# Batch 2's projections ahead of batch 0's values: a new order for one core's attention and feed-forward kernel

## The chip, the cores and the metric

The kernel runs on one core of a Trainium2 chip. The metric is device time in microseconds (us) of one execution, taken as a median over runs. Profile rows come from one profiled execution; us in them count from the start of its span.

## What is computed

Four batches (B = 4) of 512 tokens, H = 512. Each goes through cross-attention and then a feed-forward block whose weights and activations are rounded to 8-bit integers with one shared exponent per 32 numbers:

```python
query  = ctx @ Wq.T + bq ; key = ctx @ Wk.T + bk          # ctx: (4, 512, 256), 128 wide
attn   = softmax(query @ key.T)                           # (512, 512) per batch
x      = x + layernorm(x) @ attn.T                        # x: (4, 512, 512)
h      = bf16(layernorm(layernorm(x)) * ln_w + ln_b)
h      = bf16(quant(h) @ quant(W1).T + b1)                # 2048 wide
h      = bf16(gelu(h))
h      = bf16(quant(h) @ quant(W2).T + b2)                # 512 wide
out    = x + bf16(bf16(layernorm(x)) + h)
```

## The kernel before, in words

Each engine has a hand-written program; semaphores are the only order between them. A batch's tokens are 4 tiles of 128 rows (`t`), its attention 4 tiles of 128 x 512. Names are (batch, tile). The steps that matter, by engine:

- **TensorE (PE).** `context(b)` (L724) transposes the context; ScalarE's `context(b)` copies it out. `queries_keys(b)` (L732) makes both projections, 8 fp32 matmul rows of the profile; ScalarE's `query_key(b, a)` copies each out with its bias. `energies(b, t)` (L742) makes one tile of scores in one of two PSUM buffers and so waits for the `exp` of the tile two before. `values(b, t)` (L749) makes one output tile of the attention: 12 f16 matmuls (high and low parts) and an fp32 one (L761); its tile 0 waits for the transposes of all four attention tiles of the batch, each tile for the transpose of x's tile. `keep_busy(n)` (L709) multiplies the identity by itself into an unused buffer.
- **VectorE (DVE).** `negmax(b, t)` (L1031) takes the row maximum of an energy tile; `recip` and `recip_scaled` (L1036, L1040) the softmax's scale; `p_low` and `x_low` (L1045, L1050) the low halves of attention and x; `x_stats` mean and variance. Between these it quantizes the weights, one 128 x 2048 unit of W1 and of W2 per batch: `w_amax` (L862), `w_over` (L905), `w_clip`, `w_mult` (L922). The order is written out in `first_front`, `front(b, ...)` and `back(b, ...)`: first_front, back(0), front(1), back(1), then a wait for both layer norm rows (`dve.wait_ge(ld_ln, 32)`), then front(2) and the rest. The rows are first used in back(2), by `times_w` (L1059) and `plus_b` (L1064).
- **ScalarE (ACT).** `exp`, `x_high` and `p_high` make the high halves; `x_plus(b, t)` (L541) moves a tile of values out of PSUM; `x_sum(2, t)` and `x_square(2, t)` make batch 2's statistics; `load_w1(u)` and `load_w2(u)` (L533, L537) start the 1 MB loads of the next weight unit on ACT's own DMA queue, each when `w_over` of the unit before is done.
- **SP.** Issues the other DMAs in a written order: loads, then for each batch `front(b)` (L249): eight transposes, `x_transpose` (L236, waits for `x_low` of the tile and, from batch 1 on, for the batch before's `values` of that tile) and `p_transpose` (L242, waits for `p_low`), then `w2_transpose(b - 1)` and `w1_transpose(b)` (L272, L278), which wait for `w_mult`. SP takes one after the other: what stands behind a waiting issue waits too.
- **POOL (GpSimd).** Small factors, and in the second half residual sums.

Before the change PE's order around batch 1 is: energies (0,2) and (0,3), queries_keys(1), energies (1,0) and (1,1), context(2), values(0,0), energies(1,2), values(0,1), energies(1,3), values (0,2) and (0,3), queries_keys(2), energies (2,0) and (2,1). The two layer norm rows (256 KB each, one row broadcast to 128 partitions) are loaded on SP right behind the first weight unit, before `load_ctx(2)`.

Of the kernel before, what the change touches and what calls it, by code (L numbers as in the profile page):

```python
# [15 lines left out]
P = 128  # L16
# [13 lines left out]
def xattn_ffn_kernel(nc, x, ctx_in, wq, bq, wk, bk, ln_w, ln_b, w1, b1, w2, b2, out):  # L30
    B, L, H = x.shape
# [4 lines left out]
    LT = L // P  # L36
    NT = N // P
# [18 lines left out]
    with ExitStack() as stack:  # L56
# [20 lines left out]
        lnw = sb("lnw", [P, H], F32)  # L77
# [144 lines left out]
        def _(sp):  # L222
# [26 lines left out]
            def front(b, ctx=None, later=None):  # L249


                x_transpose(b, 0)
                if ctx is not None:
                    load_ctx(ctx)
                p_transpose(b, 0)
                x_transpose(b, 1)
                p_transpose(b, 1)
                x_transpose(b, 2)
                p_transpose(b, 2)
                p_transpose(b, 3)  # L260
                x_transpose(b, 3)
                if later is not None:
                    load_x(later)
                if b < B - 1:
                    if b > 0:
                        w2_transpose(b - 1)
                    w1_transpose(b)
                else:
                    w1_transpose(b)
                    w2_transpose(b - 1)  # L270
# [12 lines left out]
            load_x(1)  # L283
            load_x(2)
            sp.dma_start(wst[:, W2, :], w2_t[0]).then_inc(ld_w2, 16)
            sp.dma_start(lnw[:, :], ln_w.rearrange("(o n) -> o n", o=1).broadcast_to([P, H])).then_inc(ld_ln, 16)
            sp.dma_start(lnb[:, :], ln_b.rearrange("(o n) -> o n", o=1).broadcast_to([P, H])).then_inc(ld_ln, 16)
            load_ctx(2)
            front(0)
            load_x(3)  # L290
            front(1, 3)
            front(2)
            front(3)

# [190 lines left out]
        def _(act):  # L485
# [78 lines left out]
            def v_sums(b, t):  # L564

                if t >= 2:
# [5 lines left out]
                act.activation(vs[:, LT * b + t, :], vs[:, LT * b + t, :], ACT.Copy,  # L572
                               accum_out=sums[:, 1, 0, t:t + 1]).then_inc(v_sum, 1)

            def batch(b, front, qk, v):

                for t in range(LT + 1):
                    if t < NT and (t > 0 or front == 0):  # L580
                        exp(front, t)
                        x_high(front, t)
                    if t > 0:
                        p_high(front, t - 1)
                    if b is not None and t > 1:
                        x_plus(b, t - 2)
                    if v is not None and t == 1:
                        v_out(v, 0)
                    if v is not None and t > 0:
                        v_sums(v, t - 1)  # L590
                    if v is not None and 0 < t < LT:
                        v_out(v, t)
                    if t == 2 and b is not None:
                        load_w2(front)
                    if qk is not None and t == 3:
                        context(qk)
                if front + 1 < B and b is not None:
                    load_w1(front + 1)
                if b is not None:
                    x_plus(b, LT - 1)  # L600
                if b is None:
                    act.wait_ge(w_first, 1)
                    load_w1(front + 1)
                    x_sum(2, 0)
                    x_sum(2, 1)
                if qk is not None:
                    query_key(qk, 0)
                if b is None:
                    x_sum(2, 2)
                if b is not None:  # L610
                    x1_square(b, 0)
                if qk is not None:
                    query_key(qk, 1)
                if b is None:
                    x_sum(2, 3)
                    for t in range(LT):
                        x_square(2, t)
                if b is not None:
                    x1_square(b, 1)
                    x1_square(b, 2)  # L620
                if front + 1 < B:
                    exp(front + 1, 0)
                    x_high(front + 1, 0)
                if b is not None:
                    x1_square(b, 3)

            context(0)
            act.wait_ge(ld_bqk, 32)
            query_key(0, 0)
            query_key(0, 1)  # L630
            batch(None, 0, 1, None)
            batch(0, 1, 2, None)
            for b in range(1, B - 2):
                batch(b, b + 1, b + 2, b - 1)
# [73 lines left out]
        def _(pe):  # L708
# [55 lines left out]
            def batch(b, front, qk):  # L764


                if qk is not None and b is not None:
                    context(qk)
                for t in range(LT):
                    if b == 0:  # L770
                        values(b, t)
                    if t < NT - 2:
                        energies(front, t + 2)
                    if b is not None and b > 0:
                        values(b, t)
                if qk is not None:
                    queries_keys(qk)
                    energies(qk, 0)
                    energies(qk, 1)

            context(0)
            keep_busy(3)
# [1 line left out]
            energies(0, 0)  # L784
            energies(0, 1)
            context(1)
            batch(None, 0, 1)
            pe.wait_ge(c_idx, 1)
            batch(0, 1, 2)
            for b in range(1, B - 2):  # L790
                batch(b, b + 1, b + 2)
            batch(B - 2, B - 1, None)
# [492 lines left out]
```

## Time and profile before

| what | us |
|---|---|
| median of 3 runs | 273.22 |
| lowest and highest of them | 271.6, 274.33 |
| the profiled execution, whole | 274.33 |
| its span, first to last instruction | 272.5 |

The span and the 1.83 us around it make the profiled execution's time. It is the highest of the three runs, so differences are worked out on its rows and then added to the median. TensorE's mean granted clock in it was 0.948 of full speed (2.4 GHz); the other level is half of that, 1.2 GHz.

### The profile page before, as it was taken

The page shows a single profiled execution, that of the slowest core. Times are in us where ns is not written, and L with a number is a line of the kernel's source. Part 1 is how long each engine was busy: PE and PEld are TensorE (multiplying, and loading weights), DVE is VectorE, ACT ScalarE, POOL GpSimd, SP SyncE. Part 2 cuts the span into 40 slices and gives each one's busy share as a digit, 9 for nine tenths or more (in the row PEclk, how much of TensorE's full clock was granted, in tenths as well). Part 3 has the DMA queues.
Part 4 walks back from the last instruction along what each step waited for, and adds up shares of the span by engine and source line. Part 5 has one row for each costly group of instructions (what it writes and reads, how often), then busy time and mean ns, then how long its engine had stood idle before and what let it go on. Part 6 is the DMA issues. An engine that isn't in the chain of part 4 may idle for free.

```text
span 272.5 us, 3187 instructions
## 1 busy us (share of the span) xinstructions
PE 226.3 (83%) x931; PEld 97.5 (36%) x940; DVE 243.0 (89%) x354; ACT 175.7 (64%) x303; POOL 68.1 (25%) x101
## 2 busy tenths in 40 slices
PE   6774859989995937559996797899999789999993
PEld 6432314434431413214442333344444234444431
DVE  3599964999999999999979999999999999877982
ACT  2377753669997739767789798855556554556510
POOL 2193200042007300160521200633203333333400
PEclk9996868999999986968999999999999999999999
DMA  5999999999899828693060522656650566655773
GB/s 153 373 400 291 247 163 265 285 224 224 161 262 224 165 40 219 128 195 78 0 117 0 96 49 50 110 122 135 135 132 20 119 135 140 135 129 118 157 183 123
DMA packets 103078, 42.92 MB, mean 157 GB/s; under 512 B 93845, under 2 KB 96153, under 8 KB 102553
## 3 DMA queue, kind: packets, MB, share of 16 engines
q1 hardware_dynamic: 100224, 36.45, 61.0%
q10 hardware_dynamic: 2360, 6.30, 7.5%
q0 software_dynamic: 480, 0.02, 0.1%
q8 instruction: 5, 0.08, 0.1%
q14 instruction: 9, 0.07, 0.1%
HBM read 15.48 MB, written 4.19 MB: 72 GB/s over the span
## 4 chain that ended last, share of the span: by engine, by line
DVE 50%; PE 24%; DMA 10%; ACT 7%; issue 3%; SPq 3%; POOL 2%; ACTq 0%; DVEq 0%; POOLq 0%
DVE amax L862 12%; PE ps L821 9%; PE ps L811 5%; PE ps L758 5%; DMA pT<-phl 4%; DVE pf L976 4%; DVE wquant L966 4%; DVE w_int L905 3%; DVE phl L1047 3%; DMA xhl<-pf 3%; DVE vw L1059 3%; DVE hq L1064 3%; DVE xhl L1052 3%; DVE wquant L971 2%; DVE nmax L1033 2%
## 5 line engine op out<-in xcount | busy, mean ns | idle before, releaser
L821 PE MATMUL ps<-w2T,xhl 128*128 128x512 bf16 x247 | 56.5, 379 | 8.3 <-DMA xhl<-pf 7.9
L811 PE MATMUL ps<-w1T,cxT 128*128 128x512 bf16 x256 | 58.0, 380 | 0.0
L641 ACT ACTIVATE wst<-ps 128x1024 bf16<-128x1024 f32 x32 | 32.0, 1017 | 24.3 <-PE ps L811 24.3
L862 DVE TENSOR_REDUCE amax<-phl 128x64 f32<-128x2048 bf16 x16 | 36.5, 2281 | 4.0 <-ACT phl L648 4.0
L821 PEld LDWEIGHTS ps<-w2T,xhl 128*128 128x128 bf16 x256 | 24.4, 98 | 39.0 <-DMA xhl<-pf 8.3
L811 PEld LDWEIGHTS ps<-w1T,cxT 128*128 128x128 bf16 x256 | 23.7, 98 | 32.6 <-issue 6.2
L758 PE MATMUL ps<-h1q,xT 128*128 128x512 f16 x96 | 26.5, 435 | 9.8 <-ACT xs L546 6.2
L648 ACT ACTIVATE phl<-wst 128x2048 bf16<-128x2048 bf16 x16 | 30.6, 1910 | 1.6 <-DVE wquant L966 0.5
L758 PE MATMUL ps<-pT,xT 128*128 128x512 f16 x96 | 24.5, 410 | 7.5 <-DMA pT<-phl 7.0
L471 POOL TENSOR_TENSOR wst<-wst,vs 128x512 bf16<-128x512 bf16 x12 | 15.3, 1275 | 53.2 <-DVE wquant L971 53.2
L506 ACT ACTIVATE pf<-ps,nmax 128x512 f32<-128x512 f32 x16 | 10.8, 678 | 19.5 <-DVE nmax L1033 19.4
L661 ACT ACTIVATE wst<-ps 128x512 bf16<-128x512 f32 x16 | 9.5, 596 | 19.8 <-PE ps L821 19.4
L738 PE MATMUL ps<-cxT,wqkT 128*128 128x512 f32 x32 | 17.1, 683 | 5.6 <-ACT cxT L496 5.6
L746 PE MATMUL ps<-qkT 128*128 128x512 f32 x32 | 16.5, 618 | 5.7 <-ACT qkT L500 3.3
L758 PEld LDWEIGHTS ps<-h1q,xT 128*128 128x128 f16 x96 | 10.2, 109 | 27.0 <-issue 19.9
L407 POOL TENSOR_SCALAR mean<-sums 128x4 f32<-128x4 f32 x4 | 1.9, 479 | 69.5 <-ACT xs L546 69.5
L966 DVE TENSOR_TENSOR wquant<-phl,mxi 128x2048 int16<-128x2048 bf16 x15 | 18.3, 1223 | 0.3
L976 DVE TENSOR_TENSOR pf<-wquant,mxs 128x2048 bf16<-128x2048 int16 x15 | 18.3, 1217 | 0.0
L862 DVE TENSOR_REDUCE amax<-wst 128x64 f32<-128x2048 f32 x8 | 18.2, 2280 | 0.0
L758 PEld LDWEIGHTS ps<-pT,xT 128*128 128x128 f16 x96 | 9.7, 103 | 23.2 <-issue 14.5
L761 PE MATMUL ps<-xs,ident_x 128*128 128x512 f32 x32 | 16.7, 603 | 0.0
L905 DVE TENSOR_TENSOR w_int<-wst,mxi 128x2048 int16<-128x2048 f32 x7 | 16.0, 2284 | 0.0
(90 smaller groups left out, 370.6 us busy)
## 6 DMA issues: line engine op xcount, KB each, us to landing
wst<-in_L_ffn_W ACTq DMA_DIRECT2D x6, 1024.0 KB, 6.5
xs<-in_x SPq DMA_DIRECT2D x4, 1024.0 KB, 8.0
out_x<-wst SPq DMA_DIRECT2D x16, 256.0 KB, 2.9
cx<-in_ctx SPq DMA_DIRECT2D x4, 512.0 KB, 5.7
wst<-in_L_ffn_W SPq DMA_DIRECT2D x2, 1024.0 KB, 11.3
xhl<-pf SPq DMA_TRANSPOSE x17, 4.3
lnw<-in_L_ffn_ln_w SPq DMA_DIRECT2D x1, 256.0 KB, 12.6
lnb<-in_L_ffn_ln_b SPq DMA_DIRECT2D x1, 256.0 KB, 12.2
```

What stands on the lines that cost most here:

```text
L641: act.activation(ys[:, k, 1024 * g:1024 * g + 1024], ps_y[:, 2 * g:2 * g + 2, :], ACT.Copy)\
L648: act.activation(gs[:, k, :], ys[:, k, :], ACT.Gelu_apprx_tanh).then_inc(g_rdy, 1)
L738: last = pe.matmul(ps_qk[:, a, :], wqkT[:, a, c, :], cxT[:, c, :], start=(c == 0), stop=(c == CT - 1))
L746: pe.matmul(ps_e[:, t % 2, :], qkT[:, 0, P * t:P * t + P], qkT[:, 1, :], start=True, stop=True).then_inc(e_ps, 1)
L758: pe.matmul(ps_pv[:, t % 2, :], xT[:, t, NT * a + n, :], pTs[b % 2][:, :, NT * c + n, :], start=(s == 0), stop=False)
L761: pe.matmul(ps_pv[:, t % 2, :], ident_x[:, :], xs[:, LT * b + t, :], start=False, stop=True).then_inc(pv_ps, 1)
L811: last = pe.matmul(ps_y[:, c, :], h1T[:, k, t, :], w1T[:, 4 * c:4 * c + 4, t, :], start=False, stop=(t == KT - 1))
L821: last = pe.matmul(ps_z[:, k, :], h2T[:, k, t, :], w2T[:, t, :], start=False, stop=(t == FT - 1))
L862: dve.tensor_reduce(amax[:, a, :], by_block, AX_X, ALU.max, apply_absolute_value=True)\
L905: dve.tensor_tensor(blocks(w_int[:, :]), blocks(wst[:, a, :]), inverse, ALU.mult)\
L966: dve.tensor_tensor(pairs(h2u[:, k, :]), pairs(gs[:, k, :]), per_block(mxi[:, k, :, :]), ALU.mult).then_inc(h2_step[k], 1)
L976: dve.tensor_tensor(pairs(h2q[:, k, :]), pairs(h2u[:, k, :]), per_block(mxs[:, k, :, :]), ALU.mult).then_inc(h2_step[k], 1)
```

## The change

1. PE: a list written out, `first_batches()`, takes the place of the first two calls of `batch`. `keep_busy(22)` comes behind energies(0,3). queries_keys(2) comes ahead of values(0,0), and so does energies(1,2); energies(1,3) follows values(0,0); energies (2,0) and (2,1) are laced into the last values of batch 0. The wait for the scaled identity (`c_idx`) moves to the front of the list.
2. ACT: `first_batch()` makes ScalarE's `context(2)` right behind query_key(1,1); exp, x_high of (1,0) and (1,1) and p_high(1,0) come ahead of the four `x_square(2, t)`; `query_key(2, 0)` and `(2, 1)` come behind x_plus(0,1), with a new wait for energies(1,3).
3. SP: the loads of `lnw` and `lnb` move from ahead of `load_ctx(2)` to behind `front(1, 3)`, that is behind `w1_transpose(1)`. VectorE's wait for them stays where it is, ahead of its front(2).

```diff
--- before.py
+++ after.py
@@ -283,12 +283,12 @@
             load_x(1)
             load_x(2)
             sp.dma_start(wst[:, W2, :], w2_t[0]).then_inc(ld_w2, 16)
-            sp.dma_start(lnw[:, :], ln_w.rearrange("(o n) -> o n", o=1).broadcast_to([P, H])).then_inc(ld_ln, 16)
-            sp.dma_start(lnb[:, :], ln_b.rearrange("(o n) -> o n", o=1).broadcast_to([P, H])).then_inc(ld_ln, 16)
             load_ctx(2)
             front(0)
             load_x(3)
             front(1, 3)
+            sp.dma_start(lnw[:, :], ln_w.rearrange("(o n) -> o n", o=1).broadcast_to([P, H])).then_inc(ld_ln, 16)
+            sp.dma_start(lnb[:, :], ln_b.rearrange("(o n) -> o n", o=1).broadcast_to([P, H])).then_inc(ld_ln, 16)
             front(2)
             front(3)
 
@@ -572,17 +572,43 @@
                 act.activation(vs[:, LT * b + t, :], vs[:, LT * b + t, :], ACT.Copy,
                                accum_out=sums[:, 1, 0, t:t + 1]).then_inc(v_sum, 1)
 
+            def first_batch():
+
+                for t in range(LT + 1):
+                    if t < NT:
+                        exp(0, t)
+                        x_high(0, t)
+                    if t > 0:
+                        p_high(0, t - 1)
+                    if t == 3:
+                        context(1)
+                act.wait_ge(w_first, 1)
+                load_w1(1)
+                x_sum(2, 0)
+                x_sum(2, 1)
+                query_key(1, 0)
+                x_sum(2, 2)
+                query_key(1, 1)
+                context(2)
+                x_sum(2, 3)
+                exp(1, 0)
+                x_high(1, 0)
+                exp(1, 1)
+                x_high(1, 1)
+                p_high(1, 0)
+                for t in range(LT):
+                    x_square(2, t)
+
             def batch(b, front, qk, v):
 
 
-
                 for t in range(LT + 1):
-                    if t < NT and (t > 0 or front == 0):
+                    if t < NT and t > int(b == 0):
                         exp(front, t)
                         x_high(front, t)
-                    if t > 0:
+                    if t > int(b == 0):
                         p_high(front, t - 1)
-                    if b is not None and t > 1:
+                    if t > 1:
                         x_plus(b, t - 2)
                     if v is not None and t == 1:
                         v_out(v, 0)
@@ -590,45 +616,34 @@
                         v_sums(v, t - 1)
                     if v is not None and 0 < t < LT:
                         v_out(v, t)
-                    if t == 2 and b is not None:
+                    if t == 2:
                         load_w2(front)
-                    if qk is not None and t == 3:
+                    if b == 0 and t == 3:
+                        act.wait_ge(e_ps, 2 * NT)
+                        query_key(2, 0)
+                        query_key(2, 1)
+                    if b > 0 and qk is not None and t == 3:
                         context(qk)
-                if front + 1 < B and b is not None:
+                if front + 1 < B:
                     load_w1(front + 1)
-                if b is not None:
-                    x_plus(b, LT - 1)
-                if b is None:
-                    act.wait_ge(w_first, 1)
-                    load_w1(front + 1)
-                    x_sum(2, 0)
-                    x_sum(2, 1)
-                if qk is not None:
+                x_plus(b, LT - 1)
+                if b > 0 and qk is not None:
                     query_key(qk, 0)
-                if b is None:
-                    x_sum(2, 2)
-                if b is not None:
-                    x1_square(b, 0)
-                if qk is not None:
+                x1_square(b, 0)
+                if b > 0 and qk is not None:
                     query_key(qk, 1)
-                if b is None:
-                    x_sum(2, 3)
-                    for t in range(LT):
-                        x_square(2, t)
-                if b is not None:
-                    x1_square(b, 1)
-                    x1_square(b, 2)
+                x1_square(b, 1)
+                x1_square(b, 2)
                 if front + 1 < B:
                     exp(front + 1, 0)
                     x_high(front + 1, 0)
-                if b is not None:
-                    x1_square(b, 3)
+                x1_square(b, 3)
 
             context(0)
             act.wait_ge(ld_bqk, 32)
             query_key(0, 0)
             query_key(0, 1)
-            batch(None, 0, 1, None)
+            first_batch()
             batch(0, 1, 2, None)
             for b in range(1, B - 2):
                 batch(b, b + 1, b + 2, b - 1)
@@ -764,19 +779,35 @@
             def batch(b, front, qk):
 
 
-                if qk is not None and b is not None:
+                if qk is not None:
                     context(qk)
                 for t in range(LT):
-                    if b == 0:
-                        values(b, t)
                     if t < NT - 2:
                         energies(front, t + 2)
-                    if b is not None and b > 0:
-                        values(b, t)
+                    values(b, t)
                 if qk is not None:
                     queries_keys(qk)
                     energies(qk, 0)
                     energies(qk, 1)
+
+            def first_batches():
+
+                energies(0, 2)
+                energies(0, 3)
+                keep_busy(22)
+                queries_keys(1)
+                context(2)
+                energies(1, 0)
+                energies(1, 1)
+                queries_keys(2)
+                energies(1, 2)
+                values(0, 0)
+                energies(1, 3)
+                values(0, 1)
+                values(0, 2)
+                energies(2, 0)
+                values(0, 3)
+                energies(2, 1)
 
             context(0)
             keep_busy(3)
@@ -784,9 +815,8 @@
             energies(0, 0)
             energies(0, 1)
             context(1)
-            batch(None, 0, 1)
             pe.wait_ge(c_idx, 1)
-            batch(0, 1, 2)
+            first_batches()
             for b in range(1, B - 2):
                 batch(b, b + 1, b + 2)
             batch(B - 2, B - 1, None)
```

## Rows read from the trace of the kernel before

**Rows 1.** The page: busy time by engine; DMA share in 40 slices of the span.
```profile
PE 226.3 (83%) x931; PEld 97.5 (36%) x940; DVE 243.0 (89%) x354; ACT 175.7 (64%) x303; POOL 68.1 (25%) x101
...
DMA  5999999999899828693060522656650566655773
```
**Rows 2.** Waits of DVE, whole span: us in total, times, longest.
```profile
DVE nmax L1033 <- PE ps L746: 5.2, 1, 5.2
...
DVE rinv L1038 <- ACT pf L506: 0.6, 1, 0.6
DVE phl L1047 <- ACT phl L512: 0.6, 1, 0.6
```
**Rows 3.** Timeline of PE, 0 to 60: start, duration, what, idle before it.
```profile
4.85 1.23 PE L712 MATMUL ps<-ident 128*128 128x128 f32 x8
...
24.00 6.20 PE L738 MATMUL ps<-cxT,wqkT 128*128 128x512 f32 x8 [5.08 <-ACT cxT L496]
...
37.41 5.28 PE L758 MATMUL ps<-h1q,xT 128*128 128x512 f16 x12 [3.58 <-DMA h1q<-phl]
...
55.91 3.60 PE L738 MATMUL ps<-cxT,wqkT 128*128 128x512 f32 x8
```
**Rows 4.** Windows: busy us of PE, PEld, DVE, ACT, POOL; TensorE's granted clock, DMA share, GB/s.
```profile
24.00:30.20 6.20, 6.20 (x8) 2.34 (x8) 6.17 (x16) 3.24 (x8) 0.00 (x0) 0.59 1.09 262
37.41:43.64 6.23, 6.23 (x15) 2.63 (x16) 1.83 (x5) 0.56 (x1) 0.00 (x0) 0.57 1.20 207
...
8.00:24.00 16.00, 9.45 (x33) 4.29 (x31) 13.92 (x29) 10.47 (x19) 9.60 (x19) 0.95 1.06 387
```
**Rows 5.** Timeline of DVE: negmax (1,0), (1,2), (1,3); w_mult(W1,1), w_amax(W1,2), w_mult(W1,2).
```profile
33.02 0.68 DVE L1033 TENSOR_REDUCE nmax<-ps 128x1 f32<-128x512 f32 x1
...
44.54 0.69 DVE L1033 TENSOR_REDUCE nmax<-ps 128x1 f32<-128x512 f32 x1 [5.23 <-PE ps L746]
...
48.93 0.68 DVE L1033 TENSOR_REDUCE nmax<-ps 128x1 f32<-128x512 f32 x1
...
58.07 1.23 DVE L922 TENSOR_TENSOR wquant<-w_int,mxs 128x2048 bf16<-128x2048 int16 x1
...
63.52 2.29 DVE L862 TENSOR_REDUCE amax<-wst 128x64 f32<-128x2048 f32 x1
...
83.81 1.20 DVE L922 TENSOR_TENSOR wquant<-w_int,mxs 128x2048 bf16<-128x2048 int16 x1
```
**Rows 6.** Timeline of SP: lnw, lnb, x_transpose(1,3), w1_transpose of units 1, 2 and 3.
```profile
10.23 1.25 SPq L286 DMA_DIRECT2D lnw<-in_L_ffn_ln_w  x1
11.52 0.64 SPq L287 DMA_DIRECT2D lnb<-in_L_ffn_ln_b  x1
...
58.72 4.30 SPq L239 DMA_TRANSPOSE xT<-xhl  x1
...
64.91 3.25 SPq L274 DMA_TRANSPOSE w1T<-wquant  x1
...
89.11 2.78 SPq L274 DMA_TRANSPOSE w1T<-wquant  x1
...
117.44 2.50 SPq L274 DMA_TRANSPOSE w1T<-wquant  x1
```
**Rows 7.** DMA issues: KB each, us from issue to landing; the last is x_transpose(1,3).
```profile
wst<-in_L_ffn_W ACTq DMA_DIRECT2D x6, 1024.0 KB, 6.5
...
out_x<-wst SPq DMA_DIRECT2D x16, 256.0 KB, 2.9
...
xT<-xhl SPq DMA_TRANSPOSE x1, 6.5
```
**Rows 8.** Timeline of ACT: the issue of load_w1(2).
```profile
56.74 0.39 ACTq L535 DMA_DIRECT2D wst<-in_L_ffn_W  x1
```
**Rows 9.** DMA busy share in tenths, 30 to 50 and 50 to 70, slices of 0.5 us.
```profile
DMA  9799999899999999979900997999939964999959
...
DMA  9948969899399999967799999199999999999989
```

## The prediction

> **What bounds the kernel now.** I read the page first: DVE is busy 89% of the span, and the 16 DMA engines, though a mean over the whole span hides it, nearly all of the first third [rows 1]. Next the waits of DVE, because an engine this full sets the end wherever it does not wait. Up to the second half it has one large hole, 5.2 us at a negmax that waits for energies; two small ones of 0.6 us follow, one for an exp of batch 1 and one for a p_high of batch 2 [rows 2]. From PE's timeline the hole is plain: energies(1,2) stands behind values(0,0), and that waits for batch 0's attention transposes until 37.41 [rows 3]. It then runs at a granted clock of 0.57, mostly the lower level of 1.2 GHz, after 3.58 us of idle: 6.23 us from 37.41 to 43.64 [rows 4]. The chain of waits says the same: transposes, values, energies, negmax, and from there DVE nearly without a break to the feed-forward half. So what moves DVE's work behind 40 us moves the end, one for one.
>
> The second thing to see is SP and the DMA queue. Weight loads on ACT's queue and transposes on SP's hold each other up: a 1 MB weight load takes 6.5 us, and x_transpose(1,3), issued 2 us after load_w1(2) [rows 8], held SP for 4.30 us and landed after 6.5 us [rows 6, 7]. The change puts two loads behind these and leaves DVE's wait for them where it was.
>
> **Part 1: the energies in front.** energies(1,2) needs exp(1,0), whose negmax runs at 33.02 [rows 5], so it can be done at about 35 if PE has the projections of batch 2 behind it by then. DVE asks for it, without the hole, at 44.54 - 5.23 - 0.6 = about 38.7. The two holes of 5.23 and 0.61 us go: 5.84 us [rows 2], and ACT's exp(1,0), no longer behind four x_square, is what closes the small one.
>
> Next late would be energies(1,3), now behind values(0,0). DVE wants it 48.93 - 44.54 = 4.4 us after negmax(1,2) (p_low, x_low and a w_over lie between) [rows 5], at 43.1. values(0,0) can begin at 35.9 to 37.4 (transposes landing as before, or 1.4 us sooner, part 3) and takes about 6.23 x 0.57 = 3.6 us at the full clock, or 6.2 as now: its end is 39.5 to 43.6, and energies(1,3) follows at once. So it costs nothing warm and up to 1.5 us cold. I take nothing, by the next part.
>
> **Part 2: identities and batch 2's projections.** 22 identities at 1.23/8 = 0.154 us are 3.4 us [rows 3]. They lie in PE's 5.08 us wait for the copied context and delay nothing; at half the clock they would take 6.8 and push the projections by 1.7. What they may give: queries_keys(1) took 6.20 us at a granted clock of 0.59, while the same eight rows take 3.60 warm [rows 3, 4]. Those 2.6 us do not reach DVE by themselves, since negmax(1,0) stands behind a w_amax until 33.02. They make room for queries_keys(2), which moves in front of energies(1,2). If both are warm, PE is through them by about 33.6, ahead of exp(1,0). If the clock stays low, they end near 39, energies(1,2) comes at 40 and energies(1,3) at 47: DVE waits again for 1.5 and then some 2.7 us. Value taken: warm, 0; bounds 0 and 4.2. The new ACT wait for energies(1,3) stands behind exp(1,3), which needs that tile anyway, so it is met when reached; queued behind it are query_key(2) and p_high(1,3), which DVE needs only for its last p_low of the stage. The moved wait for the scaled identity is met before PE gets there. Both: 0.
>
> **Part 3: the rows loaded later.** In front they leave 0.5 MB fewer in a stretch that moves 387 GB/s [rows 4]: 0.52/387 = 1.4 us, by which the first transposes can land sooner. DVE does not wait for those any more: 0, from 0 to -1.4 for PE. Their two issues (1.89 us) end long before SP's next wait opens: 0.
>
> Behind, all counts. DVE ends w_mult(W1,1) at 59.2 (the next instruction's start) and reaches the wait for the rows at 63.5, 4.3 us later [rows 5]. SP passes w1_transpose(1), which needs the same w_mult, at 64.91 + 3.25 = 68.16, that is 9.0 us after it, because x_transpose(1,3) and w2_transpose(0) had to get through beside the load of W1 first [rows 6]. Then lnw's issue, 1.25, and 256 KB from lnb's issue to landing. For that I take 2.9, a store of the same size [rows 6, 7]. Landing is 9.0 + 1.25 + 2.9 = 13.2 us after w_mult, and DVE has been waiting since 4.3: a new stall of 8.9 us. All of this moves with DVE (w_mult and, through w_over, the W1 load that blocks the queue), so the 5.84 does not shorten it. Behind the waiting DVE instruction stands all of front(2): w_amax, x_low, negmax(2,2), and so ACT's exp(2,2), SP's transposes of batch 2, PE's values(2).
>
> Bounds of the stall: with the shortest w1 transpose issue (2.50) right after w_mult, lnb's 0.64 for each issue and 2.9 to land, 2.50 + 0.64 + 2.9 = 6.0, less 4.3: 1.7 us. At the other end the landing takes 6.5, as a transfer beside a weight load does [rows 7]: 8.9 + 3.6 = 12.5. I stay with 8.9, since this very queue state is in the trace.
>
> One more term: the DMA engines must do the same work in less time. Between 40 and 70 the half-us digits leave about 4 us idle, 1.0 of it at 40 to 41 [rows 9]; with the 1.4 us from the front that is 5.4 us of slack for a shift of 5.84. I put 0.6 us on the landing, bounds 0 and 3.
>
> The Trainium skill speaks against this part. In "DMA: Bandwidth & Descriptors", section Rules for kernel authors, it advises to issue a DMA early and to wait on its semaphore late; the old place does, and the new one issues late for a wait that did not move. Its section Issuing engines are not separate DMA queues says that DMAs of all issuing engines share the same 16 DMA engines, which agrees with the 6.5 us of a transpose beside ACT's load [rows 7]. Its figures in Anatomy of one DMA, fitted to transfers issued by GpSimd (2.0 us fixed plus bytes over 436 GB/s), would make an estimate of 2.6 us for lnb, and the sum 0.3 us smaller.
>
> **Sum.** -5.84 + 8.9 + 0.6 = +3.7; the 0.6 us hole of batch 2 goes too, since ACT is ahead after DVE's stall: -0.6. That is +3.1 us, 277.4 for the profiled execution's 274.33. That execution is 1.1 us over the median, so the forecast is 273.22 + 3.1 = 276.3. I count on nothing later to absorb it: what DVE waits for after that hangs on its own p_low and x_low of batches 2 and 3.
>
> **Rivals.**
> 1. *Faster: the queue is clear when w_mult ends.* The rows decide from the point where lnb lands within 4.3 + 5.84 = 10.1 us of w_mult(W1,1); forecast is 13.8. For it: a lone w1 transpose takes 2.50, and PE is through values(0) earlier than it must be. Against it: every 1 MB load on ACT's queue has a blocked transpose beside it. At the lower bound, -5.84 + 1.7 = -4.1: 269.1; halfway, 271.
> 2. *Even: the backlog is that of batch 2.* There w_mult ended at 85.0 and w1_transpose at 89.11 + 2.78 = 91.9, 6.9 us later instead of 9.0 [rows 5, 6]. Then 3.1 - 2.1 = +1.0: 274.2.
> 3. *Slower still: PE stays cold, or the landing is long.* queries_keys(2) ahead of values(0,0) becomes a load on the path: up to 4.2 us more, or 3.6 for the landing: 279.9 to 280.5. For it: clock 0.59 and 0.57 in just these stretches [rows 4]. Against it: 22 identities close most of the idle time before them.
>
> **How the numbers follow.** A change of this kernel under 1%, 2.7 us, can hardly be told from none. Forecast's own case, 0.50: its spread of -2 to +2 about 276.3 crosses the 1% line at 275.95, so 0.30 slower and 0.20 same. Rival 1, 0.20: 0.18 faster, 0.02 same. Rival 2, 0.17, same. Rival 3, 0.13, slower. Together faster 0.18, same 0.39, slower 0.43. The range of 8 in 10 reaches into rivals 1 and 3: 269.8 to 279.5. The forecast's own range is 274.3 to 278.3.
>
> **What would show it.** Right: no wait of DVE for energies at negmax(1,2); a new one of about 9 us ahead of w_amax(W1,2), released by the DMA of lnb, with DVE's w_amax(W1,2) at 66 to 67.5; SP's lnw issue 9 us after w_mult(W1,1); queries_keys(1) and (2) at about 3.6 us with the clock at 1.0. Wrong: lnb landed when DVE comes to its wait, or a stall there of less than 5 us (rival 1); a DVE wait at negmax(1,2) or (1,3) and a clock near 0.6 in PE's 24 to 41 (rival 3).

## The result, and the profile after

The changed kernel takes 280.9 us, median of four runs, against 273.36 for the kernel before: ratio 1.0264, 95% interval 1.018 to 1.0348. The forecast was 276.3, with a range up to 279.5: the sign was right, the size not. Ratios and their intervals, here and below, leave out executions that stand apart from the rest of their kernel's; medians and ranges hold them all. The four executions run from 279.29 to 291.96, and that spread is a finding of its own (questions 1 and 3 below). The profiled execution is the lowest of them: 279.29 us, its span 277.5 against 272.5, so +5.0 where +3.1 was forecast for it. Of the other three there is no trace.

DVE's largest wait after (us in total, times, longest), and DVE's timeline with negmax (1,2) and (1,3), w_mult(W1,1) and w_amax(W1,2):

```profile
DVE amax L892 <- DMA lnb<-in_L_ffn_ln_b: 12.0, 1, 12.0
```
```profile
38.57 0.69 DVE L1063 TENSOR_REDUCE nmax<-ps 128x1 f32<-128x512 f32 x1
...
42.95 0.68 DVE L1063 TENSOR_REDUCE nmax<-ps 128x1 f32<-128x512 f32 x1
...
52.10 1.23 DVE L952 TENSOR_TENSOR wquant<-w_int,mxs 128x2048 bf16<-128x2048 int16 x1
...
69.61 2.29 DVE L892 TENSOR_REDUCE amax<-wst 128x64 f32<-128x2048 f32 x1 [12.04 <-DMA lnb<-in_L_ffn_ln_b]
```

Against [rows 5], negmax(1,2) is 44.54 - 38.57 = 5.97 us earlier, and so is w_mult(W1,1): the hole is gone and nothing took its place up to here. DVE reaches its wait for the rows at 69.61 - 12.04 = 57.57, 5.95 us ahead of before, and leaves it 69.61 - 63.52 = 6.09 us behind. About 1.1 us of that is given back later, half of it in the 0.6 us at phl of batch 2, which is gone [rows 2].

PE's timeline answers to [rows 3], its windows (columns as in [rows 4]) to the granted clock:

```profile
18.77 5.07 PE L727 MATMUL ps<-ident 128*128 128x128 f32 x44
24.06 3.67 PE L753 MATMUL ps<-cxT,wqkT 128*128 128x512 f32 x8 [0.22 <-ACT cxT L496]
...
30.33 3.60 PE L753 MATMUL ps<-cxT,wqkT 128*128 128x512 f32 x8
...
36.25 2.75 PE L773 MATMUL ps<-h1q,xT 128*128 128x512 f16 x12 [0.50 <-DMA h1q<-phl]
...
39.70 1.02 PE L761 MATMUL ps<-qkT 128*128 128x512 f32 x2
```
```profile
24.06:27.73 3.67, 3.67 (x10) 1.71 (x11) 3.63 (x9) 3.08 (x8) 0.00 (x0) 1.00 0.90 203
...
36.25:39.00 2.75, 2.75 (x13) 1.43 (x14) 2.68 (x6) 2.75 (x8) 0.00 (x0) 1.00 1.18 192
```

Both projections take 3.6 to 3.7 us, the 12 f16 matmuls of values(0,0) 2.75 us (5.28 before), at a granted clock of 1.00 (2.4 GHz). PE does what the change says.

So the loss is in the wait, and its inside is SP. SP's timeline after, from x_transpose(1,0) on; the row with x2 is the pair p_transpose (1,2) and (1,3), the row behind it the second of the pair by itself. Then x_transpose(1,0), the pair and its second in before:

```profile
39.96 1.23 SPq L239 DMA_TRANSPOSE xT<-xhl  x1
...
51.03 6.27 SPq L246 DMA_TRANSPOSE pT<-phl  x2
52.40 4.89 SPq L246 DMA_TRANSPOSE pT<-phl  x1
57.39 1.25 SPq L239 DMA_TRANSPOSE xT<-xhl  x1
58.69 2.12 SPq L280 DMA_TRANSPOSE w2T<-wquant  x1
60.85 3.26 SPq L274 DMA_TRANSPOSE w1T<-wquant  x1
64.15 0.58 SPq L290 DMA_DIRECT2D lnw<-in_L_ffn_ln_w  x1
64.78 0.43 SPq L291 DMA_DIRECT2D lnb<-in_L_ffn_ln_b  x1
```
```profile
43.74 1.23 SPq L239 DMA_TRANSPOSE xT<-xhl  x1
...
55.41 3.22 SPq L246 DMA_TRANSPOSE pT<-phl  x2
57.40 1.23 SPq L246 DMA_TRANSPOSE pT<-phl  x1
```
ACT's load_w1(2) after, beside [rows 8]:
```profile
50.76 0.39 ACTq L535 DMA_DIRECT2D wst<-in_L_ffn_W  x1
```

Read the shifts, not the times. DVE is 5.97 us earlier, and load_w1(2), which follows it, 56.74 - 50.76 = 5.98. SP is not: its front(1) begins with x_transpose(1,0), which waits for values(0,0) on PE, and that is only 43.74 - 39.96 = 3.8 us earlier. So the load of W1 comes earlier in SP's row. In both kernels one transpose is still issued in the usual time behind it (1.23 us before, 1.33 after), and the next one is held until 6.3 and 6.5 us after the load's issue. Before, the load started between the two of the pair, and the one held was x_transpose(1,3) (4.30 us [rows 6]); two transposes of weights were left, 5.1 us. After, it starts ahead of the pair, the one held is the second of the pair (4.89 us), and x_transpose(1,3) is left as well: 6.8 us. So x_transpose(1,3) starts only 1.3 us earlier than before, and w1_transpose(1) ends at 64.11, 4.05 earlier. That is 10.9 us after w_mult, where 9.0 had been taken over from before.

### The profile page after: what moved, and what is told of

Same layout as the page of the kernel before. It is cut to its first block, busy times and chain, and to the rows that moved or that the text cites. A ratio compares the mean times of both kernels' runs of the same rounds, so it can differ in the third digit from the quotient of the medians.

```text
span 277.5 us, 3276 instructions
## 1 busy us (share of the span) xinstructions
PE 234.5 (85%) x975; PEld 102.8 (37%) x984; DVE 242.7 (87%) x354; ACT 176.0 (63%) x303; POOL 67.3 (24%) x101
## 4 chain that ended last, share of the span: by engine, by line
DVE 59%; PE 19%; DMA 8%; SPq 5%; ACT 3%; issue 3%; POOL 2%; DVEq 0%; POOLq 0%; ACTq 0%
DVE amax L892 14%; PE ps L851 9%; PE ps L841 5%; DVE w_int L935 5%; DVE pf L1006 4%; DVE wquant L996 4%; DVE phl L1077 4%; DVE xhl L1082 4%; DMA xhl<-pf 3%; DVE nmax L1063 3%; DVE vw L1089 3%; DVE hq L1094 3%; DVE wquant L1001 2%; DVE wquant L952 2%; SPq L246 2%
## 5 line engine op out<-in xcount | busy, mean ns | idle before, releaser
L841 PE MATMUL ps<-w1T,cxT 128*128 128x512 bf16 x256 | 59.7, 388 | 0.0
L773 PE MATMUL ps<-pT,xT 128*128 128x512 f16 x96 | 27.8, 450 | 13.4 <-ACT xs L546 7.1
L773 PE MATMUL ps<-h1q,xT 128*128 128x512 f16 x96 | 25.6, 422 | 4.8 <-ACT xs L546 4.3
L471 POOL TENSOR_TENSOR wst<-wst,vs 128x512 bf16<-128x512 bf16 x12 | 15.4, 1284 | 53.2 <-DVE wquant L1001 53.2
L506 ACT ACTIVATE pf<-ps,nmax 128x512 f32<-128x512 f32 x16 | 10.9, 681 | 25.9 <-DVE nmax L1063 25.8
L761 PE MATMUL ps<-qkT 128*128 128x512 f32 x32 | 18.4, 676 | 7.7 <-ACT pf L506 6.0
L773 PEld LDWEIGHTS ps<-pT,xT 128*128 128x128 f16 x96 | 10.5, 112 | 32.6 <-issue 26.0
L546 ACT ACTIVATE xs<-ps,mr 128x512 f32<-128x512 f32 x16 | 10.8, 675 | 7.1 <-PE ps L776 7.1
```

Of the source, the lines that this page charges most:

```text
L471: pool.tensor_tensor(ws[:, k, :], zs[:, k, :], vs[:, i, :], ALU.add).then_inc(zv_rdy, 1)
L761: pe.matmul(ps_e[:, t % 2, :], qkT[:, 0, P * t:P * t + P], qkT[:, 1, :], start=True, stop=True).then_inc(e_ps, 1)
L773: pe.matmul(ps_pv[:, t % 2, :], xT[:, t, NT * a + n, :], pTs[b % 2][:, :, NT * c + n, :], start=(s == 0), stop=False)
L841: last = pe.matmul(ps_y[:, c, :], h1T[:, k, t, :], w1T[:, 4 * c:4 * c + 4, t, :], start=False, stop=(t == KT - 1))
```

## The experiments

| run | what | executions | median, range (us) | ratio to before, 95% |
|---|---|---|---|---|
| after_again | the kernel after | 4 | 290.57, 284.64–293.79 | 1.0644, 1.0559–1.0728 |
| rows_front | after, rows at their old place | 10 | 272.49, 270.29–273.07 | 0.9928, 0.9899–0.9956 |
| rows_only | before, rows late | 4 | 278.93, 278.12–280.31 | 1.0191, 1.0128–1.0253 |
| wait_late | after, DVE's wait late | 6 | 278.68, 274.28–279.75 | 1.0206, 1.0155–1.0257 |
| old_order_wait_late | before, rows and wait late | 4 | 270.31, 270.23–271.16 | 0.9888, 0.9856–0.992 |
| energies_only | before, energies of batch 1 in front | 6 | 271.57, 270.27–281.27 | 0.9915, 0.9876–0.9955 |
| old_order_energies_wait_late | both of these | 11 | 271.81, 269.12–281.85 | 0.9862, 0.9833–0.9892 |
| x3_late | after, load_x(3) behind the rows | 5 | 280.73, 280.19–283.64 | 1.0254, 1.0221–1.0287 |
| x3_late_wait_late | and DVE's wait late | 10 | 272.6, 270.58–284.25 | 0.9936, 0.9892–0.998 |
| w1_load_late | after, load_w1(2) later | 4 | 286.06, 280.68–288.57 | no interval |
| w1_gated | load_w1(2) behind load_w2(1), wait late | 5 | 275.23, 271.71–282.61 | 0.9915, 0.9891–0.994 |
| loads_late | after, x(3) and context(3) loaded later | 4 | 281.22, 281.01–281.59 | 1.0277, 1.0205–1.0349 |
| loads_late_wait_late | and DVE's wait late | 10 | 271.78, 269.39–273.1 | 0.9938, 0.9901–0.9976 |
| after_beside | the kernel after | 6 | 288.75, 285.44–293.98 | 1.0591, 1.054–1.0643 |
| loads_late_beside | loads_late, same chip as after_beside | 6 | 280.81, 278.57–281.52 | 1.0274, 1.0224–1.0324 |
| loads_late_wait_late_beside | same chip | 12 | 271.53, 268.32–273.11 | 0.9908, 0.9868–0.9948 |
| rows_front_no_ident | rows_front without identities | 4 | 270.44, 269.59–271.89 | 0.9874, 0.9832–0.9916 |
| best_loads_late | and x(3), context(3) later | 4 | 269.81, 268.98–271.08 | 0.986, 0.9781–0.994 |

### Question 1: the rows or the new order?

**after_again**: nothing edited.

> The changed kernel once more, as the measure for the others. Its median was 7.5 us over before, while the two profiled spans differ by 5.0 (277.5 against 272.5). Theory A (all of the loss is DVE's 12.0 us wait for lnb, and the rest of the change gains 5.9): 278.5 to 281, with a DVE wait for lnb of 11 to 13 us. Theory B (the new order costs something besides, which the profiled execution shows less than others): 280 to 282.

290.57 us: above both ranges, and four executions over 9 us. In the trace of the lowest, 284.64 us, the wait for lnb is 16.5 us, and both weight loads of this stretch take 11 us instead of 6.7, with transposes beside them at up to 15.4 us instead of 7.4. This state of long loads and long transposes is called the jam below. The size of the loss is not one number.

**rows_front**: after, the two rows back where they were.

```diff
+            sp.dma_start(lnw[:, :], ...)
+            sp.dma_start(lnb[:, :], ...)
             load_ctx(2)
             front(0)
             load_x(3)
             front(1, 3)
-            sp.dma_start(lnw[:, :], ...)
-            sp.dma_start(lnb[:, :], ...)
```

> The changed kernel with the two layer norm loads back at their old place. Theory A: the wait of 12.0 us goes, holes of 0.6 and 0.4 us on DVE come back: 267 to 269, DVE at w_amax(W1,2) at about 57.6. Theory B: no wait for lnb either, but the end is at 271 to 274, since the order of PE and ACT loses elsewhere.

272.49, faster than before by 0.7%, as theory B had it. The whole loss hangs on the rows. But of the 5.84 us that PE's order takes out of DVE's first hole only some 2 reach the end: new waits for energies of 1.25 and 2.68 us, and 0.86 for an exp, come behind it:

```profile
44.00 0.69 DVE L1063 TENSOR_REDUCE nmax<-ps 128x1 f32<-128x512 f32 x1 [1.25 <-PE ps L761]
...
70.14 0.69 DVE L1063 TENSOR_REDUCE nmax<-ps 128x1 f32<-128x512 f32 x1 [2.68 <-PE ps L761]
```

**rows_only**: before, the rows alone moved (the same lines, the other way).

> The kernel before with nothing but the two loads moved behind w1_transpose(1). Theory A: SP passes w1_transpose(1) at 68.2 as in the kernel before, and 0.6 + 4.8 us later lnb is there: a DVE wait of 10 us from 63.5 to 73.6, 282 to 284. Theory B (the stall needs the crowd that the new order makes in the queue): a wait under 6 us, 276 to 279.

278.93, slower by 1.9%: the wait is near that of theory A, the time in the range of theory B. DVE's waits and values(0,0) on PE (timelines, its window with the granted clock), then SP:

```profile
40.55 0.69 DVE L1033 TENSOR_REDUCE nmax<-ps 128x1 f32<-128x512 f32 x1 [1.05 <-PE ps L746]
...
68.88 2.29 DVE L862 TENSOR_REDUCE amax<-wst 128x64 f32<-128x2048 f32 x1 [9.28 <-DMA lnb<-in_L_ffn_ln_b]
...
36.05 2.75 PE L758 MATMUL ps<-h1q,xT 128*128 128x512 f16 x12 [2.02 <-DMA h1q<-phl]
...
36.05:38.80 2.75, 2.75 (x13) 1.42 (x14) 2.75 (x3) 2.13 (x5) 0.00 (x0) 1.00 1.76 188
```
```profile
51.05 3.59 SPq L246 DMA_TRANSPOSE pT<-phl  x2
54.74 4.30 SPq L239 DMA_TRANSPOSE xT<-xhl  x1
...
60.99 2.51 SPq L274 DMA_TRANSPOSE w1T<-wquant  x1
```

Two things to see. The 5.2 us hole [rows 2] is down to 1.05 with PE's order untouched: with half a megabyte fewer in front of them the transposes let values(0,0) start at 36.05 instead of 37.41, after 2.02 us of idle instead of 3.58, and it then ran at a granted clock of 1.00 (2.75 us for 5.28). The earlier start is worth 1.4 us of this, the clock 2.5. And the wait is 9.28, close to the 8.9 that the forecast took from before: in the old order SP does move with DVE. There x_transpose(1,0) starts at 39.75 and load_w1(2) at 52.75, both 3.99 us earlier than before. The load starts between the two of the pair again, x_transpose(1,3) is held for the same 4.30 us, and w1_transpose ends 8.3 us after w_mult. The other traces without the jam say the same of the lag: where the load came forward by more than x_transpose(1,0), by 2.6 us in energies_only, 4.0 in rows_front_no_ident and 4.4 in rows_front (all with the rows in front), it is 11.7, 11.3 and 13.1 us.

**wait_late**: after, DVE's wait put behind its front(2), nothing on SP changed.

```diff
-            dve.wait_ge(ld_ln, 32)
             front(2, ...)
+            dve.wait_ge(ld_ln, 32)
```

> The changed kernel, loads late as it has them, but DVE's wait for them moved behind front(2), right ahead of their first use. Theory A: the loads land at about 69.5, DVE wants them about 22 us after 57.6, so no wait is left: 267 to 269, as with the loads in front. Theory B: 271 to 274.

278.68 (274.28 to 279.75), above both ranges. Three executions are at 279.5 to 279.8, which the ratio of 1.0206 stands for, three at 274.3 to 277.8. The wait for the rows is gone, and in the trace of the lowest DVE waits for a weight load instead (4.18 us once): the loads of this stretch took 10.4 and 11.3 us. So the long loads are not made by the two row loads themselves, which are issued behind them at 70, or by DVE standing still.

### Question 2: what is each part worth without the wait?

**old_order_wait_late**: before, with both of the moves above (rows late, wait late), PE and ACT as before.

> The kernel before with the rows loaded late, and DVE's wait moved to their first use. With the rows moved alone the 5.2 us hole had shrunk to 1.05, since values(0,0) began 1.4 us sooner and at full clock. Theory C: this gain stays if the wait goes, 269 to 271. Theory A (only PE's order closes the hole for good): 272 to 274.

270.31, all runs within 0.9 us, as theory C had it: faster than before by 1.1%, with none of PE's and ACT's new order. **energies_only** does nothing but swap two calls of PE in the old order:

```diff
-                    if b == 0:
-                        values(b, t)
                     if t < NT - 2:
                         energies(front, t + 2)
-                    if b is not None and b > 0:
+                    if b is not None:
                         values(b, t)
```

> The kernel before with energies(1,2) and (1,3) ahead of values (0,0) and (0,1) on PE, nothing else. If the hole is only the place of the energies: 5.2 us less on DVE up to 44, then the same crowd in the queue gives 2 to 4 of it back: 270 to 272. If the identities and batch 2's projections are needed for it: energies(1,3) waits behind a cold values(0,0), 272 to 274.

271.57, 0.85% faster, in the first of the two ranges; the identities and batch 2's projections are not needed for it. Both it and old_order_wait_late close the same hole of DVE, so they do not add up, as the run with both shows:

> The best so far (old order, rows late, DVE's wait at their first use, 270.3) and energies (1,2) and (1,3) ahead of values (0,0) and (0,1). DVE has 1.6 us left to win at negmax(1,2): 268.7 at the least if the queue keeps up; by theory E the weight loads come 1.6 us sooner and closer to what SP still has to do, so some executions fall back to 272 to 280.

**old_order_energies_wait_late**: 271.81 (269.12 to 281.85), ratio 0.9862. Five of its eleven executions are at 269.1 to 270.1, and others fall back as expected; the profiled one, 279.87, is among those, with load_w2(1) at 13.7 us and DVE waiting 3.43 and 4.30 us for weights. In this kernel load_w2(1) starts at 43.21, in old_order_wait_late, whose four executions have nothing of the kind, at 44.94. It pointed to that load.

### Question 3: what makes the loads long?

**x3_late** moves `load_x(3)` from behind front(0) to behind the rows; **x3_late_wait_late** also has the late wait.

> The changed kernel with one edit: batch 3's x, 1 MB that nobody needs before x_stats(3), is loaded behind the two rows instead of ahead of front(1). Theory C (the new order starts load_w2(1) while x(3) and the context of batch 3 are still in SP's queue; then the weight loads take 11 us instead of 6.5 and the transposes 12 to 15): all weight loads 6 to 7 us, SP through w1_transpose(1) by 60 to 62, lnb landed by 66 to 67, a DVE wait of 8 to 9 us, 275 to 278 with little spread. Theory D (two weight loads back to back block the transposes by themselves, x(3) does not matter): SP through at 64 to 71 as before, 279 to 291.

> As x3_late, and DVE's wait for the rows moved behind front(2), ahead of their first use. Theory C: no wait for lnb, weight loads at 6 to 7 us, so DVE keeps most of the 5.9 us: 267 to 270. Theory D: DVE waits for a weight load or for energies behind late transposes, 274 to 279 as without the x(3) edit.

280.73, in the range of theory D, and 272.6 (270.58 to 284.25), in neither: seven of its ten executions are at 270.6 to 274.2, three at 277.2 to 284.3. The wait for lnb is 15.8 us in the first one's trace, the loads 8.5 and 8.1: batch 3's x alone is not it.

**w1_load_late** starts load_w1(2) behind the last x1_square of batch 0, so that the two weight loads do not overlap; **w1_gated** makes ACT wait for the landing of load_w2(1) first, with the late wait.

```diff
                 if front + 1 < B:
+                    if b == 0:
+                        act.wait_ge(ld_w2, 32)
                     load_w1(front + 1)
```

> The changed kernel with one edit: ACT starts load_w1(2) behind batch 0's last x1_square (at about 58) instead of at 50.8, right after load_w2(1). Theory E (transposes get through only between two weight loads; where load_w2(1) has not landed when load_w1(2) is issued, they stay stuck through both): transposes of batch 1 out by 55, SP through w1_transpose(1) by 57 to 60, lnb landed at 62 to 64, and DVE then waits for the weights until 64 to 65.5 instead of 69.6 or 75: 274 to 277, little spread. Theory F (the DMA engines are full by volume, order is nothing): 1 MB less ahead of lnb is 2.7 us, a wait until 67 to 72: 277 to 288, the same spread.

> The kernel with DVE's late wait (274 to 280 before), and one more edit: ACT waits for load_w2(1) to land before it issues load_w1(2). Theory E: the two loads never overlap, the stuck state is gone, 270 to 274 in every execution. Theory F: the gate only delays the weights, 275 to 280 again.

286.06 and 275.23: theory E missed both, though two of the second's five executions are at 271.7 and 272.0. The times lie in theory F's ranges, but its reason does not hold either. load_w2(1) took 12.0 and 13.2 us with no second load beside it. The first one's DMA view, 40 to 55 us (40 slices of 0.375 us), with the load that was issued at 43.26:

```profile
DMA  9625899679999169999991400001111197998989
GB/s 60 27 44 109 317 382 360 202 257 415 394 311 213 40 146 316 304 287 350 339 571 47 70 25 25 25 10 41 27 23 23 14 313 271 456 494 316 317 184 194
...
wst<-in_L_ffn_W ACTq DMA_DIRECT2D x1, 1024.0 KB, 12.0
```

For 3.75 us (digits 23 to 32) the 16 engines move 10 to 70 GB/s, nine of the ten digits at 0 or 1, while this load, the context load and two transposes are outstanding. It is not a matter of volume.

**loads_late** takes both of SP's plain loads (loads that only copy, without a transpose) away from the start of load_w2(1): x(3) behind the rows, context(3) from behind x_transpose(1,0) to behind x_transpose(1,2). **loads_late_wait_late** adds the late wait.

```diff
-                if ctx is not None:
-                    load_ctx(ctx)
...
+                if ctx is not None:
+                    load_ctx(ctx)
...
-            load_x(3)
             front(1, 3)
...
+            load_x(3)
```

> The kernel after, with batch 3's x load moved behind the two rows and batch 3's context load moved from behind batch 1's first x transpose to behind the third. Theory G (the long transfers need a plain load of SP's still in flight when load_w2(1) starts at 43): now only transposes are in flight beside it, every weight load takes 6 to 7 us and every transpose of batch 1 6 to 9, SP's last weight transpose of batch 1 ends at 60 to 64, VectorE's wait for the second row is 8 to 12 us and the time 276 to 280 with runs within 2 us of each other. Theory H (a weight load and transposes alone can do it): loads of 8 to 14 us in the trace, wait of 13 to 17, runs spread over 4 us or more, 280 to 290.

> The same with VectorE's wait for the rows moved behind batch 2's front. Theory G: no wait for the rows, no wait for a weight load over 1 us, 267 to 270 us with all runs within 2 us. Theory H: weight loads of 8 to 14 us, VectorE waiting 3 to 5 us for one, and runs spread from 270 to 280.

281.22 with all four executions within 0.6 us, and 271.78 (269.39 to 273.1). Of theory G the narrow spread came true, and a short load_w2(1), 5.8 us; load_w1(2) at 7.8 us, the wait of 13.8 us and the time lie above its ranges. The second lies above theory G's time: its loads take 6.0 and 8.0 us, and DVE waits 1.24 us for a weight load and 3.16 us for x(3), which this edit itself loads late. These executions came from another chip than the wide ones, so the kernel after ran once more beside them:

> The kernel after, unchanged, on the same chip and in the same call as loads_late_beside, since its earlier executions came from other chips than loads_late's. Theory G (plain loads in flight beside load_w2(1) make the long transfers): runs spread over 5 us or more, 279 to 294. Rival K (the spread belongs to the chip, not to the kernel): as wide or as narrow as loads_late_beside.

> loads_late unchanged, beside the kernel after. Theory G: all runs within 2 us of each other, 280 to 282, whatever after does beside it. Rival K: the same spread as after_beside.

> loads_late_wait_late unchanged, on the same chip. Theory G: runs within 4 us, 269 to 273, as on the other chip. Rival K: runs up to 280 where after_beside is wide.

On one chip: after 288.75 (285.44 to 293.98), loads_late 280.81 (278.57 to 281.52), with the late wait 271.53 (268.32 to 273.11). The ranges are somewhat wider than theory G had them, but a third and little over half of that of after, on the same chip: the wide spread belongs to the kernel. Issues of after_beside, from issue to landing: load_w2(1) and the p_transposes (1,0) and (1,1), with DVE's wait behind it; then load_w2(1), p_transpose(1,1) and DVE's wait in loads_late_beside:

```profile
wst<-in_L_ffn_W ACTq DMA_DIRECT2D x1, 1024.0 KB, 11.0
pT<-phl SPq DMA_TRANSPOSE x1, 11.8
...
pT<-phl SPq DMA_TRANSPOSE x1, 15.3
...
DVE amax L892 <- DMA lnb<-in_L_ffn_ln_b: 17.3, 1, 17.3
```
```profile
wst<-in_L_ffn_W ACTq DMA_DIRECT2D x1, 1024.0 KB, 5.9
...
pT<-phl SPq DMA_TRANSPOSE x1, 5.4
...
DVE amax L892 <- DMA lnb<-in_L_ffn_ln_b: 13.2, 1, 13.2
...
50.65 7.54 SPq L246 DMA_TRANSPOSE pT<-phl  x2
```

The last line is what stays when the jam is gone: the pair held for 7.54 us beside load_w1(2). So the time on this chip has three pieces, each with a run: the jam, 288.75 - 280.81 = 7.9 us (the first profiled execution, with loads of 6.8 and 6.6 us, shows none); the wait, 280.81 - 271.53 = 9.3 us; and what is left is a gain of 1.8 us. Which of the two plain loads does it, and why it strikes in some executions only, stays open. A plain load in flight is not enough by itself: in rows_front_no_ident context(3) and load_w2(1) are issued together at 42.69, and nothing is long (7.4 and 6.2 us); in rows_front x(3) is in flight when load_w2(1) starts at 43.26, and the load takes 5.4 us, its ten executions within 2.8 us of each other. Nor is it shown that before is free of the jam: one of its 13 executions beside loads_late took 281.72, without a trace.

### Question 4: the identities

**rows_front_no_ident** is rows_front without `keep_busy(22)`; **best_loads_late** is that with both plain loads late.

> The changed kernel with the rows back in front (272.5 before) and without the 22 identities. If the identities carry part of the gain: queries_keys(1) takes 6 us again, energies(1,2) comes at 39 to 40 behind queries_keys(2), DVE waits there and at negmax(1,3): 274 to 277. If not: 271 to 273.5.

> The kernel after with the rows back at their old place, without the identity multiplies, and with both plain loads of batch 3 late. Theory G: 267 to 269.5 us, runs within 2 us, no hole of VectorE above 2 us. Theory H: 270 to 273, since nothing that the loads cost is taken away.

270.44, a little below the range for "if not", and 269.81, between the two theories; ratios 0.9874 and 0.986. rows_front, with the identities, was at 0.9928; its interval overlaps that of the first, so it is shown that the identities are not needed, not that they cost time. PE's timeline of rows_front, then without them, with the window of values(0,0) in each:

```profile
23.78 3.67 PE L753 MATMUL ps<-cxT,wqkT 128*128 128x512 f32 x8
...
37.81 4.44 PE L773 MATMUL ps<-h1q,xT 128*128 128x512 f16 x12 [2.34 <-DMA h1q<-phl]
...
37.81:42.25 4.44, 4.44 (x13) 1.86 (x14) 4.34 (x9) 3.70 (x10) 0.00 (x0) 0.62 1.02 190
```
```profile
23.68 5.97 PE L753 MATMUL ps<-cxT,wqkT 128*128 128x512 f32 x8 [4.96 <-ACT cxT L496]
...
37.71 2.75 PE L773 MATMUL ps<-h1q,xT 128*128 128x512 f16 x12 [1.00 <-DMA h1q<-phl]
...
37.71:40.46 2.75, 2.75 (x13) 1.42 (x14) 2.65 (x9) 2.75 (x9) 0.00 (x0) 1.00 1.14 210
```

The identities save 2.3 us on the first projection and give them back: PE is done early, idles 2.34 us ahead of values(0,0), and runs that at a clock of 0.62 after it. Without them the slower projection fills this time, the idle is 1.00 us, and the 12 f16 matmuls of values(0,0) are done 1.8 us sooner (40.46 for 42.25). Where the time of waiting is fixed by a transfer, filling the first gap only moved it to the next. energies_only agrees: without identities its first projection takes 6.52 us, the idle ahead of values(0,0) is 0.44 us, and the 12 matmuls take 2.75. In these traces DVE's later waits for energies are 3.9 us with them, 1.7 without. The late loads make no measurable difference on top. best_loads_late, rows_front_no_ident and old_order_wait_late are the best versions here, 1.4, 1.3 and 1.1% below before; their intervals overlap, so which is the fastest is open, and the last changes far less.

## Why the prediction was right or wrong

**Part 1, right at its place.** Forecast -5.84 at negmax(1,2); measured -5.97 there and -5.95 at the wait. Next late, energies(1,3), came as worked out: PE wrote it by 40.7, DVE wanted it at 42.95. The sentence before the parts, that DVE's work moves the end one for one, was too strong: where no wait follows (rows_front) about a third of the 5.84 is left, since new holes for energies and an exp open behind it.

**Part 2, right in sum, one term mis-sized.** Warm projections, 0 on the path: measured so. The 22 identities took 5.07 us, not 3.4: each is two rows of the profile (44), and I had priced one row each. They fit into PE's wait all the same (0.22 us of it left). What the forecast did not ask is whether the kernel needs them; question 4 says no.

**Part 3, the step that failed: "All of this moves with DVE".** I took SP's lag of 9.0 us behind w_mult from before and moved it along with DVE. It hangs on two engines: load_w1(2) follows DVE (-5.98), but SP's row of transposes begins when values(0,0) on PE frees the buffer (-3.8). Where the two shifts are equal (rows_only) the lag is 8.3, a little under the 9.0; that the whole stall of 9.28 comes so close to the forecast's 8.9 is partly luck, since the landing, at 4.2 instead of 2.9, makes up for the shorter lag. Where they are not equal, the load falls one transpose earlier in SP's row, and one more is left behind the held one. By terms, for the first profiled execution: lag 10.87 for 9.0, lnw's issue with the gaps around it 0.67 for 1.25, lnb's landing 4.8 for 2.9 + 0.6; 10.87 + 0.67 + 4.8 - 4.33 = 12.0, against 9.5. That is the difference of 2.5 at the wait. The landing was priced by a store of the same size; the row loads took 3.3 to 5.8 us in the traces that have them behind the transposes.

**The 0.6 us for the queue, bounds 0 to 3: too small, and of the wrong kind.** I had treated the DMA engines as a matter of volume. What came in some executions is a jam with engines partly idle, 7.9 us in the median on one chip, and gone when SP's plain loads are away from the start of load_w2(1). How much of it is in the measured median of 280.9 is open, since only the lowest execution has a trace, and that one has no jam. It is not all of the miss: without the jam the two medians of loads_late, 280.81 and 281.22, are above the range too (with x(3) and context(3) at another place).

**The front of part 3, "DVE does not wait for those any more: 0".** True in the changed kernel, as the energies are already ahead of values(0,0). But rows_only shows that moving the rows alone closes 4.2 of the 5.2 us, because values(0,0) starts 1.4 us sooner and then runs at a granted clock of 1.00. Moving the rows and reordering PE both close the same hole, so one of the two was enough, and the rows brought the wait with them.

**The rivals.** Rivals 1 and 2 (lnb landed early; lag of 6.9) are ruled out by the 10.9. Rival 3 joined two causes: PE stayed warm (granted clock 1.00), so that half is wrong. Of the long landing, 3.6 us over, some 1.3 us came (4.8 for 2.9 + 0.6). Its time, 279.9 to 280.5, is near the measured median of 280.9 by luck, as the longer lag and the spread are not in it.

The Trainium skill's advice, in "DMA: Bandwidth & Descriptors", section Rules for kernel authors, to wait on a DMA's semaphore late is borne out here: in loads_late_beside, with the rows where the change put them and only DVE's wait moved, the time falls from 280.81 to 271.53.

## What to carry to other kernels

A stall that is read from the old trace can be moved as a whole only if everything in it follows the same engine: list for each instruction in the chain what releases it, and shift each by its own releaser. When a load is issued later, move its wait too, to where the data is first used. And before adding work that fills an engine's gap, ask whether the gap behind it is set by something else; here it only moved the idle time, with the lower clock, to a place nearer the path.

## What was not expected of the hardware

- Two 1 MB loads on ACT's queue took 6.8 and 6.6 us in one execution and 11.0 and 12.0 in another of the same program (after and after_beside), with transposes of batch 1 beside them at 3.4 to 7.4 us and up to 15.3. In w1_load_late the 16 engines moved 10 to 70 GB/s for 3.75 us while four transfers were outstanding. What starts it was not found; with two plain loads issued later neither trace of loads_late has it.
- SP's issue instructions themselves block: a transpose's issue takes 1.23 us where nothing holds it, one of them 4.89 us and a pair 7.54 us beside a weight load.
- Two broadcast rows of 256 KB each, with 0.6 us between their issues and little beside them but the last weight transpose, took 3.5 and 4.8 us to land (a store of that size 2.9 [rows 7]).
